# A two-layer expert network around attention: the head's loads, choices and ranks in another order

## What is computed

```python
logits = einsum('btd,ed->bte', x, gate_w) + expert_bias      # 12 experts
topk_logits, topk_idx = top_k(logits, 2)
topk_w = softmax(topk_logits)
h = silu(einsum('btd,efd->btef', x, w1))                     # 8 experts, 128 -> 256
y = einsum('btef,edf->bted', h, w2)                          # 256 -> 128
out = einsum('bte,bted->btd', w_ffn, y) + w_zero * x         # experts 8 to 11 return x
```

## Time and profile before

| | |
|---|---|
| median of 3 runs | 989.55 us (989.32 to 990.73) |
| the profiled execution | 991.01 us, of which the span is 989.2 us |
| busy: PE | 905.8 us, 92% of the span, 12732 matmuls |
| busy: PEld | 649.6 us |
| busy: DVE | 740.3 us, 75% |
| busy: ACT | 588.3 us, 59% |
| busy: POOL | 573.5 us, 58% |
| mean granted TensorE clock | 0.967 |

### The profile page before, as it was taken

The page is one execution under the profiler, slowest core; times in us unless marked ns, Lnnn a source line. Parts: engine busy times, 40 slices in busy tenths (PEclk is TensorE's granted clock), DMA queues, the critical chain, the costliest instruction groups (busy, mean ns, idle before and its releaser), DMA issues.

```text
span 989.2 us, 33646 instructions
## 1 busy us (share of the span) xinstructions
PE 905.8 (92%) x12732; PEld 649.6 (66%) x12732; DVE 740.3 (75%) x2092; ACT 588.3 (59%) x1108; POOL 573.5 (58%) x658
## 2 busy tenths in 40 slices
PE   7688899799999999999999999999999999987993
PEld 6587645489755555556995555558975558945993
DVE  6859489773599999999558999997429885485464
ACT  3434756545677766666558777665567765575631
POOL 4573767730157566654105777764136776777775
PEclk8799879989999999999999999999999999999997
DMA  8825557266344432224552222236652238926745
GB/s 255 256 48 122 157 144 220 63 127 139 104 124 132 121 93 81 62 77 92 123 144 71 81 74 83 75 87 120 156 143 70 75 85 149 220 61 118 176 111 138
DMA packets 203580, 118.19 MB, mean 119 GB/s; under 512 B 98560, under 2 KB 194399, under 8 KB 203296
## 3 DMA queue, kind: packets, MB, share of 16 engines
q1 hardware_dynamic: 188320, 89.40, 34.8%
q0 software_dynamic: 15104, 26.65, 10.8%
HBM read 35.07 MB, written 64.26 MB: 100 GB/s over the span
## 4 chain that ended last, share of the span: by engine, by line
PE 69%; DVE 10%; issue 8%; POOL 4%; DMA 4%; ACT 3%; SPq 2%; ACTq 0%; POOLq 0%; DVEq 0%
PE banks L613 15%; PE banks L749 11%; PE banks L778 8%; PE banks L724 7%; PE banks L572 4%; PE banks L573 3%; PE banks L574 3%; DVE row_max L1624 3%; ACT probs L1035 2%; PE banks L716 2%; POOL big L1136 2%; PE banks L518 2%; PE banks L789 2%; DMA big<-yg,slots 2%; PE banks L857 2%
## 5 line engine op out<-in xcount | busy, mean ns | idle before, releaser
L1624 DVE TENSOR_REDUCE row_max<-banks 128x2 f32<-128x512 f32 x512 | 338.6, 683 | 78.7 <-PE banks L749 75.7
L1035 ACT ACTIVATE probs<-banks 128x512 f32<-128x512 f32 x512 | 278.0, 595 | 133.7 <-PE banks L749 131.5
L1136 POOL DMA_INDIRECT big<-yg,slots x236 | 228.8, 970 | 210.7 <-PE banks L749 58.1
L1122 POOL DMA_INDIRECT xg<-xs,slots x236 | 235.9, 1000 | 113.8 <-issue 75.1
L613 PE MATMUL banks<-w_all,h_f 128*128 (+1 forms) x1600 | 211.3, 277 | 2.6 <-DVE x_all L1489 2.6
L613 PEld LDWEIGHTS banks<-w_all,h_f 128*128 128x128 f32 x1600 | 195.1, 193 | 6.1 <-issue 3.3
L943 ACT ACTIVATE h_f<-banks 128x512 f32<-128x512 f32 x200 | 119.3, 597 | 131.9 <-PE banks L574 130.0
L778 PE MATMUL banks<-probs,v_op 128*32 128x256 f32 x2048 | 168.6, 384 | 0.6 <-ACT probs L1035 0.6
L749 PE MATMUL banks<-band_parts,thirds 96*32 96x296 bf16 (+2 forms) x4096 | 167.7, 276 | 0.0
L724 PE MATMUL banks<-q_op,k_op 32*128 32x256 bf16 x1024 | 121.6, 275 | 17.1 <-issue 7.4
L749 PEld LDWEIGHTS banks<-band_parts,thirds 96*32 96x32 bf16 x4096 | 95.0, 96 | 56.2 <-issue 56.2
(11 more groups left out here) (176 smaller groups left out, 1271.6 us busy)
## 6 DMA issues: line engine op xcount, KB each, us to landing
yg<-y_rows SPq DMA_DIRECT2D x77, 256.0 KB
q_in<-kq_kept SPq DMA_DIRECT2D x96, 64.0 KB
k_op<-kq_kept SPq DMA_DIRECT2D x96, 64.0 KB
xg<-zeros SPq DMA_DIRECT2D x5, 896.0 KB
kq_kept<-kq_hi SPq DMA_DIRECT2D x32, 128.0 KB
kq_kept<-kq_lo SPq DMA_DIRECT2D x32, 128.0 KB
xg<-zeros SPq DMA_DIRECT2D x1, 3968.0 KB
xg<-zeros SPq DMA_DIRECT2D x2, 1984.0 KB
```

Source lines behind the costliest of these rows:

```text
L1035: act.activation(probs[:, four % 2, u % 4, :], banks[:, ST[u % 2], :], ACT.Exp).then_inc(A["exp_done"], 1)
L1122: pool.indirect_dma_start(xg[q], bass.IndirectOffsetOnAxis(slots[:, q % 4, c, t:t + 1], 0), xs[:, NTH[q] % 2, t, :], None, bounds_check=CA ...
L1136: pool.indirect_dma_start(y_back[:, i, c, :], None, yg[q], bass.IndirectOffsetOnAxis(slots[:, q % 4, c, t:t + 1], 0)).then_inc(gathered[i] ...
L1624: dve.tensor_reduce(row_max[:, gp, :, qt, j], banks[:, MX[(16 * b + v) % 3], :].rearrange("p (k c) -> p k c", k=2), AX.X, ALU.max).then_in ...
```

## The change

1. SP issues x of segment 2 and the clearing for segment 0 right behind w1, ahead of w2 and of the twelve attention loads; a clearing starts with its small yg part. The clearing waits for `zeros_ready`, the first POOL fill, in place of `pool_set`.
2. `chosen` is laid out expert by expert with a leading zero column. DVE runs a scan over it (`tensor_tensor_scan`, 348 elements, `go_on` is 0 at each expert's first column and 1 elsewhere), which gives for each tile the counts of all earlier tiles of that partition (`earlier`). The ranks are two matmuls: ones by `earlier` (348 columns) and triangle by `chosen`. This holds for every routed segment.
3. PE turns two chunks of segment 2 at groups 9, 10 and 12 of the dense segment (`COLS`), gates two at 10, 11 and 13 (`GATES`), the first of each pair ahead of the group's second layer. ACT follows.
4. DVE's order in the dense part is written out: the first sums come ahead of segment 2's statistics; rows, splits and the two choices lie between the sums, the first choice ahead of the sums of groups 12 and 13, the second ahead of 14 and 15. `band_constants` moves behind segment 2's and the first batch's attention work, and ACT no longer waits for it.
5. Segment 2's ranks are counted at group 3 of segment 0's experts (before: 6), `weigh` at 2 (before: 5), and projections, values and transposes of the first batches one group earlier.
6. POOL scatters seven tiles of segment 0 ahead of segment 2's root (before: six), ten tiles of segment 2 ahead of the first gather (before: nine), and so one tile fewer later. Segment 2's scatter waits for its splits by chunk.

```diff
@@ -160,7 +160,8 @@
-    BESIDE = 9
+    COLS = {9: (0, 1), 10: (2, 3), 12: (4, 5)}
+    GATES = {10: (0, 1), 11: (2, 3), 13: (4, 5)}
@@ -220,7 +221,9 @@
         hot1 = sb("hot1", [P, TS, E])
-        chosen = sb("chosen", [P, TS * E], BF16)
+        chosen = sb("chosen", [P, E, TS + 1], BF16)
+        earlier = sb("earlier", [P, E, TS + 1], BF16)
+        go_on = sb("go_on", [P, E, TS + 1], BF16)
         gap = sb("gap", [P, TS])
@@ -357,12 +360,12 @@
             def clear(n, i, part=0):
+                if part == 0:
+                    sp.dma_start(yg_all[n, i][n * GS:n * GS + 16, :],
+                                 zeros[0:16, :].bitcast(F32)).then_inc(zero_in[n, i], 16)
                 rows = xg_all[n, i].rearrange("(n p) c -> p n c", p=P)
...
                 sp.dma_start(rows[:, part * k:part * k + k, :], bc(zeros[:], 1, k)).then_inc(zero_in[n, i], 16)
-                if part:
-                    return
-                sp.dma_start(yg_all[n, i][n * GS:n * GS + 16, :], zeros[0:16, :].bitcast(F32)).then_inc(zero_in[n, i], 16)
@@ -371,6 +374,9 @@
             sp.dma_start(big[:, 0:FE * 256], w1).then_inc(w1_in, 16)
+            load_x(2)
+            sp.wait_ge(zeros_ready, 1)
+            clear(*ROOM[0])
             sp.dma_start(w_all[:].bitcast(F32).rearrange("p (e f) -> p e f", e=FE)[:, :, 256:512],
@@ -383,9 +389,6 @@
                              prior[L // 2 - 32:L // 2, L // 2 - 32 - reach:L // 2 + reach]).then_inc(attn_in, 16)
-            load_x(2)
-            sp.wait_ge(pool_set, 1)
-            clear(*ROOM[0])
             clear(*ROOM[2])
...
@@ -525,12 +532,10 @@
                     pe.wait_ge(tri_ready, 1)
-                pe.matmul(banks[:, RB, RK:RK + nt * E], tri_h[:], chosen[:, 0:nt * E], start=True, stop=False,
-                          skip_group_check=True)
-                for k in range(1, nt + 1):
-                    mm = pe.matmul(banks[:, RB, RK + k * E:RK + (nt + 1) * E], ones_h[:],
-                                   chosen[:, 0:(nt + 1 - k) * E], start=False, stop=k == nt, skip_group_check=True)
-                mm.then_inc(R["ranked_done"], 1)
+                pe.matmul(banks[:, RB, 0:E * (TS + 1)], ones_h[:], earlier[:].rearrange("p e t -> p (e t)"),
+                          start=True, stop=False, skip_group_check=True)
+                pe.matmul(ranks_of()[:, :, 0:nt], tri_h[:], chosen[:, :, 1:nt + 1],
+                          start=False, stop=True, skip_group_check=True).then_inc(R["ranked_done"], 1)
@@ -593,12 +598,13 @@
                         pe.wait_ge(w2_in, 16)
-                    if g >= 2:
-                        dense_down(q, g - 2)
-                    if nxt and BESIDE <= g < BESIDE + chunks[nxt]:
-                        turn_tokens(nxt, g - BESIDE)
-                    if nxt and BESIDE < g <= BESIDE + chunks[nxt]:
-                        gate_logits(nxt, g - BESIDE - 1)
+                    for half in range(2):
+                        if nxt and g in GATES:
+                            gate_logits(nxt, GATES[g][half])
+                        if nxt and g in COLS:
+                            turn_tokens(nxt, COLS[g][half])
+                        if g >= 2 and half == 0:
+                            dense_down(q, g - 2)
@@ -642,18 +648,18 @@
                         turn_tokens_of(0)
-                    if q == 0 and g == 6:
+                    if q == 0 and g == 3:
                         count_ranks(2)
-                    if q == 0 and g == 11:
+                    if q == 0 and g == 10:
                         pe.wait_ge(attn_pool_ready, 1)
...
                         project(0)
-                    if q == 0 and g == 12:
+                    if q == 0 and g == 11:
                         pe.wait_ge(R["xtf_ready"], K0[3])
                         values(0)
-                    if q == 0 and g == 14:
+                    if q == 0 and g == 13:
                         turn_tokens_of(1)
-                    if q == 0 and g == 16:
+                    if q == 0 and g == 15:
                         project(1)
...
@@ -987,14 +994,13 @@
                         token_cols_of(0)
-                    if q == 0 and g == 5:
+                    if q == 0 and g == 2:
                         weigh(2)
-                    if q == 0 and g == 11:
-                        act.wait_ge(attn_ready, 1)
+                    if q == 0 and g == 10:
                         high_part(0)
-                    if q == 0 and g == 14:
+                    if q == 0 and g == 13:
                         token_cols_of(1)
-                    if q == 0 and g == 16:
+                    if q == 0 and g == 15:
                         high_part(1)
@@ -1070,11 +1076,15 @@
             pool.memset(ones_h[:], 1.0)
+            pool.memset(chosen[:], 0.0)
+            pool.memset(go_on[:], 1.0)
             pool.iota(first_slot[:], pattern=[[GS, NG]], base=0, channel_multiplier=0,
...
             pool.memset(neg_half[:], -0.5)
+            pool.wait_ge(pool_set, 1)
+            pool.memset(go_on[:, :, 0:1], 0.0)
             pool.memset(q_in[:], 0.0).then_inc(pool_set, 1)
@@ -1111,12 +1121,15 @@
                 if t0 == 0:
-                    pool.wait_ge(R["split_done"], KE[q])
+                    if q != 2:
+                        pool.wait_ge(R["split_done"], KE[q])
                     pool.wait_ge(R["slots_ready"], NTH[q] + 1)
...
                 for t in range(t0, t1):
+                    if q == 2 and t % 4 == 0:
+                        pool.wait_ge(R["split_done"], KB[q] + t // 4 + 1)
                     for c in range(2):
@@ -1215,18 +1228,18 @@
             attention_constants()
-            scatter_rows(0, 0, 6)
+            scatter_rows(0, 0, 7)
             token_root_all(2)
-            scatter_rows(0, 6, 12)
+            scatter_rows(0, 7, 12)
             batch_norm(0)
             batch_norm(1)
-            scatter_rows(2, 0, 9)
+            scatter_rows(2, 0, 10)
             gather_rows(0, 0, 4)
             batch_norm(2)
-            for b, t0, t1 in ((0, 9, 12), (1, 12, 16), (2, 16, 20)):
+            for b, t0, t1 in ((0, 10, 13), (1, 13, 17), (2, 17, 21)):
                 spread(gather_rows, 0, 4 + 2 * b, 6 + 2 * b, b, 4)
                 spread(scatter_rows, 2, t0, t1, b, 4, 4)
-            spread(scatter_rows, 2, 20, 24, 3, 4)
+            spread(scatter_rows, 2, 21, 24, 3, 4)
             norm_turns(3, 4)
@@ -1371,8 +1384,11 @@
                 wait(dve, R["ranked_done"], NTH[q])
-                dve.tensor_tensor(chosen[:, 0:nt * E].rearrange("p (t e) -> p t e", e=E), hot0[:, 0:nt], hot1[:, 0:nt],
-                                  ALU.add).then_inc(R["chosen_ready"], 1)
+                link(dve.tensor_tensor(chosen[:, :, 1:nt + 1], hot0[:, 0:nt].rearrange("p t e -> p e t"),
+                                       hot1[:, 0:nt].rearrange("p t e -> p e t"), ALU.add))
+                dve.tensor_tensor_scan(earlier[:].rearrange("p e t -> p (e t)"), go_on[:].rearrange("p e t -> p (e t)"),
+                                       chosen[:].rearrange("p e t -> p (e t)"), 0.0, ALU.mult,
+                                       ALU.add).then_inc(R["chosen_ready"], 1)
@@ -1399,8 +1415,8 @@
                 dve.wait_ge(R["ranked_done"], NTH[q] + 1)
-                counts = banks[:, RB, RK + nt * E:RK + nt * E + FE]
-                link(dve.tensor_scalar(n_shift[:], counts, 1.0 / GS, (GS - 1.0) / GS - 0.5 + 0.5 / GS,
+                counts = ranks_of()[:, 0:FE, nt:nt + 1]
+                link(dve.tensor_scalar(n_shift[:].unsqueeze(2), counts, 1.0 / GS, (GS - 1.0) / GS - 0.5 + 0.5 / GS,
                                        ALU.mult, ALU.add))
@@ -1415,7 +1431,7 @@
                 nt = SEG[q][1]
-                dve.tensor_tensor(slot_e[:, 0:nt], banks[:, RB, RK:RK + nt * E].rearrange("p (t e) -> p t e", e=E),
+                dve.tensor_tensor(slot_e[:, 0:nt], ranks_of()[:, :, 0:nt].rearrange("p e t -> p t e"),
                                   bc(base[:], 1, nt), ALU.add).then_inc(R["ranks_read"], 1)
@@ -1438,6 +1454,11 @@
                         token_moments(q, k // 2)
+
+            def halves_of(q, h):
+                for k in range(2 * h, min(2 * h + 2, chunks[q])):
+                    token_stats(q, k)
+                token_moments(q, h)
@@ -1495,22 +1516,13 @@
-            def dense_experts(q, nxt=None):
+            def dense_experts(q):
...
                 for g in range(groups[q] + 3):
-                    if nxt and BESIDE - 1 <= g < BESIDE + chunks[nxt] - 1:
-                        k = g - BESIDE + 1
-                        if k >= 4:
-                            token_split(nxt, k - 4)
-                            dve.wait_ge(R["split_done"], KB[nxt] + k - 3)
-                        token_rows(nxt, k)
                     if g >= 3 and g % 2 == 1:
                         dense_sums(q, g - 3)
-                        if nxt and g == 9:
-                            batch_stats(0)
```

(48 more changed lines are left out.)

## The result

The changed kernel takes 1001.6 us (median, 998.8 to 1002.77) beside 989.43 us (988.36 to 990.73) for the one before on the same chip: a ratio of 1.0127 [1.0112, 1.0141], 12.2 us slower. The forecast was 995.7, 6.1 us slower, with a range up to 1000.5. The direction and the places were right; the loss is twice what was forecast and lies above the range. The profiled execution took 1002.21 us with a span of 1000.4 and a mean granted clock of 0.958.

What follows compares the result with a forecast made beforehand. The prediction took TensorE (PE), busy 92% of the span, as the bound. Its terms, 13.2 us lost up to X, minus 2.6 at the stop at 200.2, minus 4.5 for ranks, gave +6.1: 995.7 us, range 988 to 1000.5.

Steps and rivals of the forecast that it cites:

- Part 1: SP's new load order: last attention load at 32.6, so POOL's first scatter at 36.3, 3.5 us later than before.
- S: Start of POOL's first scatter: before 32.8, forecast 36.3.
- Part 2: Two more scatters on POOL ahead of segment 2's root, 1.28 us each: R = S + 23.7.
- Parts 3 and 4: Order from R to D, forecast 34.0 us (before 22.4), then D to X, forecast 33.5 (before 37.9).
- D: Start of segment 0's first second layer, forecast 94.0; as rival: ranks no cheaper, 1001.7, with C 0.14.
- R: Moment PE resumes with segment 2's first transpose: before 54.0, forecast 60.0.
- X: End of routed segment 0's expert blocks: before 114.3, forecast 127.5.
- Part 5: PE's stop at 200.2, ahead of segment 2's gathered columns: 2.6 of its 7.3 us go.
- C: Start of PE's first matmul on segment 2's gathered columns; as rival: loads at 37, scan 0.9, 1000.5, with D 0.14.
- Part 6: PE's ranks of segments 3 to 6: one wide matmul for each, minus 4.5 us.
- A: Rival: attention loads land in time, at 28, S about 31; 990.4 us, chance 0.2.
- B: Rival: DVE does not hold PE in the dense part; 979 to 984 us, chance 0.14.

Runs made afterwards that it cites:

- the last version: Kernel before plus new ranks, loads, attention constants behind segment 0's scatter, ten segment 2 tiles, and splits and bias constants in DVE's idle gap: 983.12 us, 0.9923.

## Why the prediction was wrong

**Part 1** held: last load at 32.15 for 32.6, S 36.59 for 36.3. The small error at S hides two: the loads were 0.45 early, and from them to S it took 4.4 for 3.7, since POOL's first constant took 1.54 us in this execution. **Part 2** held to the tenth. Its side remark, that the earlier first sum is worth nothing, is true for this kernel, but it hid a debt: the later statistics cost 2.6 us as soon as S is early (31.46, with six tiles).

**Parts 3 and 4: the slow-clock term failed.** The order of the pieces, who waits for whom, and the places of the stops were as forecast. I had counted the low clock at 0.8 (down 7 at 2.1 in place of 1.3), "+1.6" behind the fifth transpose, and "1.5 for slow clock behind the stop at D": 3.9 us. No run shows a clock term of this size; what the runs showed in its place, by taking the low clock away, is 7.4. Two errors are in it. The second layer, PE's longest piece there, takes 1.7 at the low level (granted 0.50). The 2.1 of the prediction leave it 1.2 behind a slow transpose of 0.9, which is what it took in the kernel before:

```profile
56.16 1.38 PE L613 MATMUL banks<-w_all,h_f 128*128 128x128 f32 x8
```

It starts there 2.2 us behind R, and the next transpose, at 57.38, is fast again: the granted clock went from 0.50 to 1.00 at about 56.9, within that row, while in the changed order it stands 0.9 behind R, wholly at the low level (1.91, granted 0.50 in 60.33 to 63.0). And I took the clock to be back for good 3 to 4 us behind a stop, while it fell again behind the 1.42 us stop at 66.53 (granted 0.50 in 67 to 69). In the profile of the kernel after it was back at 1.00 some 2.8 us behind the start at 60.33, 3.5 behind that at 66.53, 5.6 behind that at 78.05 and 5.5 behind D. So 3.5 of the 6.0 us at X are this term, in this profile; with the spread above it is 2.4 to 5.1.

The rest, 2.5, is small sizes: 0.3 at S, and 1.9 from R to D and 0.3 from D to X, which are the full-clock times (33.5 and 32.3) less my sums without their clock terms (31.6 and 32.0). The scan took 0.88 where I took 0.55, and the strided write of `chosen` 0.66 in place of 0.46: 0.53 of the 1.9 together. The scan of 348 elements takes 882 to 884 ns in all six places. Of my two rows, the one that I did not take (0.31 for 128 elements, so 0.85 to 0.93 for 348) was the better guide.

**Part 5** held: the stop at C fell by 2.4 (forecast 2.6). It does not stay there, though: it is 6.0 to 6.3 in the four versions with X 2.8 to 5.4 earlier, so it takes up about 1.2 of what they win, and 4.7 to 4.9 in the others with ten tiles ahead of the first gather. **Part 6**: from C to the end the profile is 5.8 shorter (4.5 forecast), but the ranks alone gave 3.2 there, and profiles differ by as much, so the size is not settled closer than that.

**The sum**: 6.0 more at X, 0.4 less won from X to C (2.2 for 2.6), 1.3 more won behind it, so the span is 5.1 above the forecast, the medians 6.1. The range failed because its upper end was made from late loads and a slow scan alone; the clock term, the least known of all, had no bounds of its own.

**The rivals.** A is dead by the first constant (32.15, not 28). C's 1000.5 and D's 1001.7 lie next to the measured 1001.6, and that is chance: C's scan of 0.9 came but its loads at 37 did not, and D's dear ranks did not come at all. B (faster) needed DVE not to hold PE; it does, at all three stops. But a clean order does exist: with the constants off the path and the sums left as they were, the new loads and ranks give 984.4 in place of 990.05. What the change lost by was the loads with POOL's constants left ahead of the scatters, one more tile ahead of the root, and its dense order with the low clock behind each stop, not its ranks. The dense order was not put back by itself in the kernel after, so its share as a whole is argued from these runs.

## What to carry to other kernels

In this kernel the second choice, put ahead of a sum that the matmul engine waits for, cost about 4.7 us at D, and the low clock behind the stops 7.4 us up to X. So price a stop with the slow stretch behind it, from rows at the low level (a second layer took 1.71 there, 0.95 at the full clock), and give that term bounds. Before a load is moved ahead of others, look at who waits for the loads that it passes; here one engine's constants, first read by PE at 116.9, some 80 us later, held the scatters that everything else waited for.

## What the runs showed that was not expected

- Matmuls on zeros in the stops made the kernel 5.2 us faster: the granted clock went from 0.65 to 0.86 in six stretches to 1.00 in all, and a second layer from 1.71 to 0.95 us.
- The clock was low again behind stops of 1.42 and 1.21 us, in a stretch between several stops; the earlier trace rows had shown it behind one of 3.07. The length of the stop alone does not tell it in these profiles: behind 0.62 us in the same place it stayed up, and so it did behind the 1.42 us ahead of the first transpose in the last version (four transposes 0.66, granted 1.00 in 52 to 56) and behind 2.45 us at 45.1 in the kernel before (second layer 1.13, granted 1.00 in 44 to 47). Among five profiles with the same program from R to the fifth transpose, that stretch took 16.8 to 20.4 us; with the matmuls on zeros it took 15.5.
- The issue behind a 1536 KB load and the one behind the 2432 KB clearing stand for 6.8 and 7.2 us; in the kernel before, where other DMAs come next, it was 7.1 and 8.2, so the wait moved with the load; the first attention load behind w2 then stands 2.1 us:

```profile
5.56 6.78 SPq L364 DMA_DIRECT2D yg<-zeros  x1
12.39 0.43 SPq L368 DMA_DIRECT2D xg<-zeros  x1
12.86 7.23 SPq L380 DMA_DIRECT2D w_all<-in_w  x1
20.13 2.07 SPq L383 DMA_DIRECT2D wstage<-in_wq  x1
```
